# Local attention of a fused network on one core: scores on quarters of the array, and four reorderings

## The chip, the core and the metric

The kernel runs on one core of a Trainium2 chip. A core has TensorE (PE in the rows: matmuls; PEld is its weight loads), VectorE (DVE), ScalarE (ACT), GpSimd (POOL) and SyncE (SP), which here only issues DMAs. The engines run their own instruction lists and wait for each other through semaphores. PE reads SBUF and writes PSUM, eight banks of 512 float32 per partition. The metric is the device time of one execution in microseconds (us).

## What is computed

The reference is a token mixer, a linear attention and two feed-forward layers with local attention. The change touches the last part:

```python
def local_attention(q, k, v):                 # 8 heads of 64, window 128
    bk, bv = (look_around(bk), look_around(bv))       # previous window and this one: 256 keys
    sim = jnp.einsum('bhwid,bhwjd->bhwij', bq, bk)
    mask = (i < j) | (i > j + WINDOW) | (j == -1)
    attn = jax.nn.softmax(jnp.where(mask, -max, sim), axis=-1)
    return jnp.einsum('bhwij,bhwjd->bhwid', attn, bv)

def _layer(x, ...):
    q, k, v = split(shift_token(x) @ wqkv)
    q, k = rotary_xpos(l2norm(q) * qs, l2norm(k) * ksc)
    x = x + local_attention(q, k, v) @ wo
    h = layernorm(shift_token(x)) * lg + lb
    a, g = split(h @ w1 + b1)
    return x + (a * gelu(g)) @ w2 + b2        # two such layers, 4096 tokens
```

A query i of a window sees the keys i to 127 of the previous window and 0 to i of its own. `shift_token` takes the second half of the channels from the token before.

## The kernel before

The 4096 tokens are 32 tiles of 128. Each of the two layers is a local phase (attention, `local_phase`, line 964) and then an MLP phase (`mlp_phase`, line 1480). In the profile the local phases stand at about 634 to 1086 us and 1298 to 1745 us, the MLP phases behind them, and the token mixer and the linear attention ahead of the first.

**The local phase** is a software pipeline written by hand: `schedule` (line 1003) writes steps 0 to 3 out, loops over steps 4 to 31 in twos, and writes three draining steps out. In step n, PE (line 1399) does in this order, where a, b, c, d say which tiles exist: q and k of tile n (`project`, fp32r as three products each, L117 to L119, 12 matmuls), the transposes of q and then k of tile n-1 (L1412, 4 each), the transposes of the probabilities of pairs of heads 0 and 1 of tile n-2 (L1375, 4 each), v of tile n-1 (6 matmuls), pairs 2 and 3, the output product of tile n-3 (12 matmuls, ends with the semaphore y_full), two transposes of the next tile's x (L1349), four of the inverse row sums (L1394), the scores of tile n-1 (L1368), and probabilities times v of tile n-2 (L1385).

Scores of a pair of heads: each head has 64 rows (dimensions) of qT and kT, so that two heads lie in the two halves of the array's rows. One matmul is 64 rows by 128 queries with 256 moving keys; its head's result goes to a bank of its own. The profile counts each float32 matmul of this kind twice: the program lists 8 a tile, the trace 16. `kT` holds two windows in two slots; the tile's own keys are in slot 1 in every other step, and in slot 0 in the others. Pairs 0 and 1 go to the banks of q and k (QK, QK+1), pairs 2 and 3 to the banks of the transposes (TQ, TQ+1).

ACT in a step (line 1132): high part of the output (L1135), v (L1139), squares of q and k (L1143), qT and kT (L1147), the four copies of transposed probabilities (L1123), the high part of the next x (`x_hi`, L1105), copies of x, and at its end eight exponentials (L1117). DVE (line 1245): the rope products (L1265, L1270), sums of squares (L1273), the residual addition (L1192, waits for y_full), the low part of the next x (`x_lo`, L1182, L1184: it lets PE project that tile), and then eight masked row maxima (`score`, L1224) with ten steps of the norms' inverse square root between them (`rnorm`, L1233 to L1241). POOL adds the rope products (L1070) and multiplies by the norms (L1075): q first, then k; these release the transposes L1412. In layer 0 `late_stats` (line 1312), 19 short dependent DVE instructions for the last eight tiles' layer norm, stands between step 3 and the loop.

**The MLP phase** works on eight groups of four tiles. The shifted half of the channels comes back from memory: SP loads it for group g+1 while group g runs (`m_shifted`, L1529). SP first issues the next layer's weights and tables (L1518, L1520, layer 0 only).

Of the kernel before, what the change touches and what calls it, by code (L numbers as in the profile page):

```python
# [963 lines left out]
def local_phase(nc, s, mem, K, A, layer):  # L964
# [12 lines left out]
        (f"l{layer}_kT", [P, 2, LPAIRS, P], F32), (f"l{layer}_v", [P, 2, LINNER], F32),  # L977
# [39 lines left out]
    with nc.Block() as block:  # L1017
# [30 lines left out]
        def _(pool):  # L1048
# [3 lines left out]
            nc.gpsimd.memset(kt[:, 1], 0.0)  # L1052
# [38 lines left out]
        def _(act):  # L1091
# [39 lines left out]
            def step(n, r, a, b, c, d, piece=None):  # L1131
# [12 lines left out]
                if b:  # L1144
                    for k, dst in enumerate((qt[:], kt[:, 1 - r])):
                        wait(act, s.qk_t, 2 * (n - 1) + k + 1)
                        nc.scalar.activation(dst.rearrange("p m t -> p (m t)"), ps[:, TQ + k],  # L1147
# [6 lines left out]
                if a:  # L1154
                    x_hi(n + 1, 1 - r)
# [20 lines left out]
        def _(dve):  # L1176
# [67 lines left out]

            def step(n, r, a, b, c, d):
# [33 lines left out]
                if d and not drain(n, 2):  # L1279
                    add(n)  # L1280
                if a:
# [5 lines left out]
                    x_lo(n + 1, 1 - r)  # L1287
                for h in range(LH):
                    if b:
# [44 lines left out]
            schedule(dve, step, rebase, loop=late_stats)  # L1334
# [10 lines left out]
        def _(pe):  # L1345
# [53 lines left out]
            def step(n, r, a, b, c, d):  # L1399
                if a or b:  # L1400
                    wait(pe, s.x_done, n + 1)
                if a:
                    wait(pe, s.turned, n)
                    wait(pe, s.masked, 4 * (n - 1) - 2)
                    project(r, 0, QK)
                    project(r, 1, QK + 1).then_inc(s.qk_full.sem, 1)
                if b:
                    wait(pe, s.masked, 4 * (n - 1))
                    for k in range(2):
# [754 lines left out]
```

## Time and profile before

| | us |
|---|---|
| time, median of 3 runs (1953.76 to 1954.8) | 1953.86 |
| the profiled execution | 1955.45 |
| its span in the trace | 1953.7 |
| PE busy | 1863.4 |
| DVE busy | 1522.5 |
| ACT busy | 1094.7 |
| POOL busy | 431.3 |

The profiled execution is 1.6 us above the median and 1.75 us above its own span. A busy PE is not PE at its peak, since matmuls overlap in the records. The mean granted PE clock was 0.984 of full speed. The rows further below give a start (us from the span's start), a duration in us, the engine, the line, what is written from what, the shape, how many were merged (x) and, in brackets, the idle time of the engine before it and who ended it.

### The profile page before, as it was taken

What the parts mean: (1) busy time and instruction counts of PE and PEld (TensorE: products, weight loads), DVE (VectorE), ACT (ScalarE), POOL (GpSimd) and SP (SyncE); (2) the same over time, 40 slices, a digit from 0 to 9 for tenths busy, and PEclk for the clock granted to TensorE, in tenths of its full rate; (3) what the DMA queues carried; (4) which work ended last, traced back from release to release, by engine and by line L of the source; (5) the groups of instructions that cost most, each with busy time, mean ns of one, the idle gap of its engine ahead of it and who ended that gap; (6) DMA issues with size and microseconds to landing.
All of it is one profiled execution on the core that took longest, in us unless ns stands there. A gap on an engine that the chain in (4) does not pass through costs nothing. (4 is left out here: it accounts for less than half of the span.)

```text
span 1953.7 us, 40490 instructions
## 1 busy us (share of the span) xinstructions
PE 1863.4 (95%) x13340; PEld 1624.6 (83%) x13340; DVE 1522.5 (78%) x4717; ACT 1094.7 (56%) x2551; POOL 431.3 (22%) x319
## 2 busy tenths in 40 slices
PE   8899999999999799999998799979999999989998
PEld 8789889899898578888887688867888888878887
DVE  6888878878687688888887577768888888867777
ACT  4433433433432578888887334427787778853333
POOL 0000000000000335444543000013544454411010
PEclk9999999999999899999999899989999999999999
DMA  9100000000010100000000200010000000000002
GB/s 342 43 1 1 1 1 1 1 1 1 11 57 1 50 7 5 5 5 5 5 4 11 85 12 11 11 44 4 6 4 5 5 5 4 5 22 12 11 11 91
DMA packets 44980, 44.46 MB, mean 23 GB/s; under 512 B 8359, under 2 KB 39387, under 8 KB 44894
## 3 DMA queue, kind: packets, MB, share of 16 engines
q1 hardware_dynamic: 44894, 43.33, 6.7%
q8 instruction: 52, 0.85, 0.2%
q14 instruction: 34, 0.28, 0.0%
HBM read 34.93 MB, written 8.39 MB: 22 GB/s over the span
## 5 line engine op out<-in xcount | busy, mean ns | idle before, releaser
L1117 ACT ACTIVATE l_probs<-l_probs,l_negmax 128x256 f32<-128x256 f32 x512 | 253.2, 496 | 64.8 <-DVE l_negmax L1224 64.8
L1075 POOL TENSOR_TENSOR l_t<-l_t,l_rnorm 128x512 f32<-128x512 f32 x128 | 131.0, 1044 | 301.7 <-DVE l_rnorm L1241 301.7
L117 PE MATMUL ps<-local_w_hi,l_xT 128*128 128x512 f32 x384 | 167.5, 436 | 25.2 <-DVE l_xT L1184 16.1
L1070 POOL TENSOR_TENSOR l_t<-l_t,l_t 128x1024 f32<-128x1024 f32 x64 | 152.6, 2384 | 146.0 <-DVE l_t L1270 146.0
L1123 ACT ACTIVATE l_probsT<-ps 128x512 f32<-128x512 f32 x256 | 138.4, 594 | 40.3 <-PE ps L1375 40.2
L118 PE MATMUL ps<-local_w_lo,l_xT 128*128 128x512 f32 x384 | 155.5, 405 | 0.0
L119 PE MATMUL ps<-local_w_hi,l_xT 128*128 128x512 f32 x384 | 154.5, 402 | 0.0
L117 PE MATMUL ps<-m_hnT_hi,ffn_w_hi 128*128 128x512 f32 (+1 forms) x352 | 143.5, 408 | 10.4 <-DVE m_u L1642 6.1
L486 ACT ACTIVATE attn_exp<-ps 128x512 f32<-128x512 f32 x128 | 76.5, 600 | 133.1 <-PE ps L119 133.1
L1375 PE MATMUL ps<-ident,l_probs 128*128 128x128 f32 x1024 | 135.2, 276 | 6.2 <-ACT l_probsT L1123 6.2
L118 PE MATMUL ps<-m_hnT_lo,ffn_w_hi 128*128 128x512 f32 (+1 forms) x352 | 140.3, 399 | 0.0
L119 PE MATMUL ps<-m_hnT_hi,ffn_w_lo 128*128 128x512 f32 (+1 forms) x352 | 140.2, 398 | 0.0
L1375 PEld LDWEIGHTS ps<-ident,l_probs 128*128 128x128 f32 x1024 | 119.2, 142 | 16.1 <-ACT l_probsT L1123 5.9
L1368 PE MATMUL ps<-l_kT,l_qT 64*128 64x256 f32 x1024 | 127.9, 389 | 2.2 <-DVE l_t L1270 2.2
L1265 DVE TENSOR_TENSOR l_t<-ps,rope_c 128x1024 f32<-128x1024 f32 x64 | 78.4, 1224 | 65.6 <-ACT l_sq L1143 57.5
L1385 PEld LDWEIGHTS ps<-l_probsT,l_v 128*64 128x64 f32 x2048 | 110.5, 137 | 21.3 <-issue 21.3
L1050 POOL MEMSET l_xT<- 128x520 f32 x2 | 1.1, 531 | 571.5 <-POOLq L450 569.6
L1385 PE MATMUL ps<-l_probsT,l_v 128*64 128x128 f32 x2048 | 125.9, 276 | 0.3 <-DVE x L1192 0.3
L1581 ACT ACTIVATE m_gelu<-ps,ffn_b 128x512 f32<-128x512 f32 x80 | 55.1, 689 | 110.2 <-PE ps L119 110.2
L117 PEld LDWEIGHTS ps<-local_w_hi,l_xT 128*128 128x128 f32 x384 | 74.4, 194 | 49.2 <-DVE l_xT L1184 17.1
L1368 PEld LDWEIGHTS ps<-l_kT,l_qT 64*128 64x128 f32 x1024 | 94.0, 186 | 21.3 <-issue 13.1
L1568 ACT ACTIVATE m_u_hi<-m_u 128x512 fp32r<-128x512 f32 x80 | 50.6, 632 | 106.2 <-DVE m_u L1642 106.2
(252 smaller groups left out, 5823.5 us busy)
## 6 DMA issues: line engine op xcount, KB each, us to landing
tok_x<-x SPq DMA_DIRECT2D x16, 512.0 KB, 8.2
m_shifted<-shifted SPq DMA_DIRECT2D x20, 256.0 KB, 2.7
shifted<-x SPq DMA_DIRECT2D x64, 64.0 KB, 1.5
out<-x SPq DMA_DIRECT2D x8, 512.0 KB, 4.5
ffn_w_raw<-ffn_w SPq DMA_DIRECT2D x6, 640.0 KB
local_w_raw<-ffn_wqkv SPq DMA_DIRECT2D x4, 768.0 KB, 5.0
tok_base<-attn_base SPq DMA_DIRECT2D x4, 512.0 KB, 8.7
h<-txt SPq DMA_DIRECT2D x4, 512.0 KB, 8.4
```

Of the source, the lines that this page charges most:

```text
L117: nc.tensor.matmul(out, wh, mh, start=start, stop=False, skip_group_check=True)
L118: nc.tensor.matmul(out, wh, ml, start=False, stop=False, skip_group_check=True)
L119: return nc.tensor.matmul(out, wl, mh, start=False, stop=stop, skip_group_check=True)
L486: nc.scalar.activation(ex[:, at % 2], ps[:, at % 2], ACT.Exp).then_inc(s.attn_exp.sem, 1)
L1070: nc.gpsimd.tensor_tensor(t1[:], t1[:], t2[:], ALU.add).then_inc(s.summed.sem, 1)
L1075: nc.gpsimd.tensor_tensor(v, v, rn[:, a * LH:(a + 1) * LH].unsqueeze(2).to_broadcast([P, LH, DH]), ALU.mult).then_inc(s.rotated.sem, 1)
L1117: last = nc.scalar.activation(v, v, ACT.Exp, bias=nb[:, h:h + 1], scale=-1.0, accum_out=rsum[:, h:h + 1])
L1123: nc.scalar.activation(pt[:, pair], ps[:, PT[pair]], ACT.Copy).then_inc(s.p_done.sem, 1)
L1265: nc.vector.tensor_tensor(t1[:].rearrange("p a (h d) -> p a h d", d=DH), q, cw, ALU.mult)
L1368: last = nc.tensor.matmul(ps[:, bank + e, at:at + 2 * P], qt[rows, pair, :], kt[rows, :, pair, :], start=True, stop=True)
L1375: last = nc.tensor.transpose(ps[:, PT[pair], k * P:(k + 1) * P], pm[:, pair, k * P:(k + 1) * P], K.ident[:])
L1385: last = nc.tensor.matmul(ps[e * DH:(e + 1) * DH, OT, pair * P:(pair + 1) * P], vv[:, w, h * DH:(h + 1) * DH], pt[:, pair, (2 * e + w) * P ...
```

## The change

Five edits.

1. `score` works on quarters of the array: 64 rows by 64 queries. Queries 0 to 63 need 192 of the 256 keys, queries 64 to 127 another 192. Where the own window is in slot 1 these are in one piece (16 matmuls of 192 keys in the program, 32 in a trace); where it is in slot 0 they are two pieces of 128 and 64 (32 matmuls, 64 in a trace). `kT` is laid out pair by pair, its two slots side by side. What isn't written holds older numbers, which the mask covers.
2. The transposes of k come behind those of the first pair of probabilities. The waits for `qk_done` and `turned` move ahead of the inverses.
3. Steps 0 and 1: x_t, x_hi and x_lo of tile 1 come earlier, v of tile 0 is projected at the head of step 1, and DVE does x_lo and the first four row maxima of step 1 ahead of the norms.
4. `late_stats` runs ahead of step 0.
5. SP loads the first shifted group ahead of the next layer's weights.

```diff
-        (f"l{layer}_kT", [P, 2, LPAIRS, P], F32), (f"l{layer}_v", [P, 2, LINNER], F32),
+        (f"l{layer}_kT", [P, LPAIRS, 2, P], F32), (f"l{layer}_v", [P, 2, LINNER], F32),
...
@@ ACT, step
+                if a and isinstance(n, int) and n == 0:
+                    x_hi(n + 1, 1 - r)
                 if a:
                     wait(act, s.qk_full, n + 1)
...
@@ DVE, step
+                if a and one_of(n, 0):
+                    x_lo(n + 1, 1 - r)
                 if a:
                     wait(dve, s.squared, n + 1)
...
+                if one_of(n, 1):
+                    x_lo(n + 1, 1 - r)
+                    for h in range(LH // 2):
+                        if h == 0:
+                            wait(dve, s.scored, 1)
+                        score(0, h, mask)
...
-            schedule(dve, step, rebase, loop=late_stats)
+            late_stats()
+            schedule(dve, step, rebase)
...
@@ PE
-            def score(half):
+            def score(half, own):
...
+                reach = (((slice(0, 3 * DH),), (slice(DH, 4 * DH),)) if own else
+                         ((slice(2 * DH, 4 * DH), slice(0, DH)), (slice(0, 2 * DH), slice(3 * DH, 4 * DH))))
                 for pair in (2 * half, 2 * half + 1):
-                    for e in range(2):
-                        rows, at = slice(e * DH, (e + 1) * DH), pair % 2 * 2 * P
-                        last = nc.tensor.matmul(ps[:, bank + e, at:at + 2 * P], qt[rows, pair, :],
-                                                kt[rows, :, pair, :], start=True, stop=True)
+                    at = pair % 2 * 2 * P
+                    for part in range(len(reach[0])):
+                        for part_of_q in range(2):
+                            qs, keys = slice(part_of_q * DH, (part_of_q + 1) * DH), reach[part_of_q][part]
+                            for e in range(2):
+                                rows = slice(e * DH, (e + 1) * DH)
+                                last = nc.tensor.matmul(ps[qs, bank + e, at + keys.start:at + keys.stop], qt[rows, pair, qs],
+                                                        kt[rows, pair].rearrange("p w t -> p (w t)")[:, keys],
+                                                        start=True, stop=True)
...
@@ PE, step
+                if second:
+                    project(1 - r, 2, V).then_inc(s.v_full.sem, 1)
...
                     project(r, 0, QK)
+                    if first:
+                        x_t(n + 1, 1 - r)
                     project(r, 1, QK + 1).then_inc(s.qk_full.sem, 1)
                 if b:
                     wait(pe, s.masked, 4 * (n - 1))
...
+                    turned_t(n - 1, 0)
                 if c:
                     probs_t(n - 2, 0)
+                if b:
+                    turned_t(n - 1, 1)
...
@@ SP, MLP phase
+            shifted(0, 0)
             if not last_layer:
                 for dst, src in K.local_loads(layer + 1):
...
+            sp.wait_ge(*s.normed.room(2, 2))
+            shifted(1, 1)
+            with sp.Fori(1, NG // 2) as p:
```

`turned_t(t, k)` is the wait for `rotated` and the four transposes that stood in the loop over k.

PE in a step of the loop, behind the projection of q and k; l_t is the rotated q (first) and k, l_probs the probabilities. Before:

```order
L1412 MATMUL ps<-ident,l_t_8239 128x128 [waits s_l0_rotated]
L1412 MATMUL ps<-ident,l_t_8239 128x128 x3
L1412 MATMUL ps<-ident,l_t_8239 128x128 [waits s_l0_rotated]
L1412 MATMUL ps<-ident,l_t_8239 128x128 x3
L961 ISA
L1375 MATMUL ps<-ident,l_probs 128x128 [waits s_l0_exped]
L1375 MATMUL ps<-ident,l_probs 128x128 x3
```

And of the changed kernel:

```order
L1399 MATMUL ps<-ident,l_t_8239 128x128 [waits s_l0_rotated]
L1399 MATMUL ps<-ident,l_t_8239 128x128 x3
L961 ISA
L1405 MATMUL ps<-ident,l_probs 128x128 [waits s_l0_exped]
L1405 MATMUL ps<-ident,l_probs 128x128 x3
L961 REGISTER_ALU
L1399 MATMUL ps<-ident,l_t_8239 128x128 [waits s_l0_rotated]
L1399 MATMUL ps<-ident,l_t_8239 128x128 x3
```

Four transposes of probabilities now stand between those of q and those of k.

PE at the end of a step of the loop, from the inverses (l_spread) to probabilities times v. Before, every step:

```order
L1394 MATMUL ps<-ident,l_spread 128x128 [waits s_l0_p_done,s_l0_spread]
L1394 MATMUL ps<-ident,l_spread 128x128 x3
L1368 MATMUL ps<-l_kT,l_qT 128x256 [waits s_l0_turned,s_l0_qk_done]
L1368 MATMUL ps<-l_kT,l_qT 128x256 x7
L1385 MATMUL ps<-l_probsT,l_v 64x128 [waits s_l0_y_done,s_l0_v_done]
```

The changed kernel, in a step with the own window in slot 1:

```order
L1424 MATMUL ps<-ident,l_spread 128x128 [waits s_l0_spread,s_l0_p_done,s_l0_turned,s_l0_qk_done]
L1424 MATMUL ps<-ident,l_spread 128x128 x3
L1391 MATMUL ps<-l_kT,l_qT 64x192 x16
L1415 MATMUL ps<-l_probsT,l_v 64x128 [waits s_l0_y_done,s_l0_v_done]
L1415 MATMUL ps<-l_probsT,l_v 64x128 x15
```

In the steps between, the row of 16 is eight rows that alternate between 64x128 x4 and 64x64 x4. The inverses carry the scores' waits too.

SP at the head of the MLP phase of layer 0. Before:

```order
L1518 DMA local_w_raw<-ffn_wqkv 128x1536 x2
L1518 DMA local_w_raw<-ffn_wo 128x4x256
L1520 DMA rope_c<-rope_cos 128x1024
L1520 DMA rope_s<-rope_sin 128x1024
L1520 DMA l_qkscale<-ffn_q_scale 128x64
L1520 DMA l_qkscale<-ffn_k_scale 128x64
L1521 UNCONDITIONAL_BRANCH
L1521 ISA
L1529 ISA [waits s_rows_stored1,s_rows_stored0,s_m0_normed]
L1529 DMA m_shifted<-shifted 128x4x128
```

And of the changed kernel:

```order
L1554 DMA m_shifted<-shifted 128x4x128 [waits s_rows_stored1,s_rows_stored0]
L1560 DMA local_w_raw<-ffn_wqkv 128x1536 x2
L1560 DMA local_w_raw<-ffn_wo 128x4x256
L1562 DMA rope_c<-rope_cos 128x1024
L1562 DMA rope_s<-rope_sin 128x1024
```

The first shifted group stands ahead of the seven loads instead of behind them.

## Rows read from the trace of the kernel before

**Rows 1.** Timeline of PE, one step of layer 0's loop.
```profile
909.79 2.00 PE L1368 MATMUL ps<-l_kT,l_qT 64*128 64x256 f32 x16
911.72 1.97 PE L1385 MATMUL ps<-l_probsT,l_v 128*64 128x128 f32 x32
913.62 0.50 PE L117 MATMUL ps<-local_w_hi,l_xT 128*128 128x512 f32 x1
...
916.51 1.09 PE L1412 MATMUL ps<-ident,l_t 128*128 128x128 f32 x8
917.44 1.04 PE L1375 MATMUL ps<-ident,l_probs 128*128 128x128 f32 x8
918.24 0.48 PE L117 MATMUL ps<-local_w_hi,l_xT 128*128 128x512 f32 x1
...
919.71 1.03 PE L1375 MATMUL ps<-ident,l_probs 128*128 128x128 f32 x8
920.50 0.36 PE L117 MATMUL ps<-local_w_hi,l_oT_hi 128*128 128x256 f32 x1
...
921.89 0.28 PE L119 MATMUL ps<-local_w_hi,l_oT_lo 128*128 128x256 f32 x1
...
922.76 2.00 PE L1368 MATMUL ps<-l_kT,l_qT 64*128 64x256 f32 x16
```

**Rows 2.** Timeline of PE in the linear attention: float32 matmuls on the whole array.
```profile
170.37 1.51 PE L848 MATMUL ps<-attn_kv,attn_qT 128*128 128x130 f32 x12
```

**Rows 3.** Timeline of DVE, the same step as rows 1.
```profile
909.36 0.42 DVE L1192 TENSOR_TENSOR x<-ps,x 128x256 f32 x1 [0.64 <-PE ps L119]
910.98 0.42 DVE L1224 CUSTOM_DVE_ANT_0 l_probs<-ps,mask_odd 128x256 f32<-128x256 f32 x1
922.33 0.42 DVE L1192 TENSOR_TENSOR x<-ps,x 128x256 f32 x1 [0.66 <-PE ps L119]
```

**Rows 4.** Timeline of ACT, the same step.
```profile
911.88 0.51 ACT L1117 ACTIVATE l_probs<-l_probs,l_negmax 128x256 f32<-128x256 f32 x1 [0.57 <-DVE l_negmax L1224]
...
918.69 1.06 ACT L1123 ACTIVATE l_probsT<-ps 128x512 f32<-128x512 f32 x2
```

**Rows 5.** Timeline of POOL, the same step.
```profile
914.85 2.05 POOL L1075 TENSOR_TENSOR l_t<-l_t,l_rnorm 128x512 f32<-128x512 f32 x2 [4.78 <-DVE l_rnorm L1241]
```

**Rows 6.** Timeline of DVE and PE, layer 0: late statistics, and who waits.
```profile
690.27 0.16 DVE L151 TENSOR_REDUCE l_rstd<-h_stats 128x8 f32<-128x16 f32 x1
...
695.05 0.17 DVE L1316 SCALAR_TENSOR_TENSOR l_shift<-l_mean,l_rstd 128x8 f32<-128x8 f32 x1
...
696.66 0.50 PE L117 MATMUL ps<-local_w_hi,l_xT 128*128 128x512 f32 x1 [3.13 <-ACT l_v L1139]
```

**Rows 7.** Timelines: first steps, DVE of layer 0, then POOL, DVE and PE of layer 1.
```profile
642.84 1.23 DVE L1265 TENSOR_TENSOR l_t<-ps,rope_c 128x1024 f32<-128x1024 f32 x1 [5.87 <-ACT l_sq L1143]
...
1315.22 2.04 POOL L1075 TENSOR_TENSOR l_t<-l_t,l_rnorm 128x512 f32<-128x512 f32 x2 [2.56 <-DVE l_rnorm L1241]
...
1320.49 1.22 DVE L1265 TENSOR_TENSOR l_t<-ps,rope_c 128x1024 f32<-128x1024 f32 x1 [5.23 <-PE ps L1412]
...
1328.03 0.47 PE L117 MATMUL ps<-local_w_hi,l_xT 128*128 128x512 f32 x1 [2.98 <-DVE l_negmax L1224]
```

**Rows 8.** Timelines: MLP phases of layers 0 and 1, SP, DVE and PE.
```profile
1090.94 1.11 SPq L1529 DMA_DIRECT2D m_shifted<-shifted  x2
...
1098.70 0.87 DVE L1613 BATCH_NORM_STATS2 m_stats<-m_shifted 128x6 f32<-128x128 f32 x4 [10.63 <-DMA m_shifted<-shifted]
...
1086.96 0.47 PE L117 MATMUL ps<-m_hnT_hi,ffn_w_hi 128*128 128x512 f32 x1 [2.14 <-PEq L1017]
...
1137.59 1.09 PE L1708 MATMUL ps<-ident,m_hn 128*128 128x128 f32 x8 [1.41 <-DVE m_hn L1621]
...
1745.86 0.47 PE L117 MATMUL ps<-m_hnT_hi,ffn_w_hi 128*128 128x512 f32 x1 [2.13 <-PEq L1017]
...
1787.95 1.09 PE L1708 MATMUL ps<-ident,m_hn 128*128 128x128 f32 x8 [0.15 <-DVE m_hn L1621]
```

More of the change, by code:

```diff
@@ L1154, in step @@
                 if a:
-                    x_hi(n + 1, 1 - r)
+                    if not (isinstance(n, int) and n == 0):
+                        x_hi(n + 1, 1 - r)
                     x_copy((n + 2) % T, r)
@@ L1243, in _, with one_of @@
             LAST = 10
+            def one_of(n, *steps):
+                return isinstance(n, int) and n in steps
             def step(n, r, a, b, c, d):
@@ L1286, in step @@
                     chain.mark(rnorm(2))
-                    x_lo(n + 1, 1 - r)
+                    if not one_of(n, 0, 1):
+                        x_lo(n + 1, 1 - r)
                 for h in range(LH):
-                    if b:
+                    if b and not (one_of(n, 1) and h < LH // 2):
                         if h % 4 == 0:
@@ L1399, in step @@
             def step(n, r, a, b, c, d):
+                first, second = (isinstance(n, int) and n == k for k in range(2))
                 if a or b:
                     wait(pe, s.x_done, n + 1)
+                if second:
+                    project(1 - r, 2, V).then_inc(s.v_full.sem, 1)
                 if a:
@@ L1408, in step @@
                     wait(pe, s.masked, 4 * (n - 1))
-                    for k in range(2):
-                        wait(pe, s.rotated, 2 * n - 1 + k)
-                        for m in range(LPAIRS):
-                            last = nc.tensor.transpose(ps[:, TQ + k, m * P:(m + 1) * P], t1[:, k, m * P:(m + 1) * P],
-                                                       K.ident[:])
-                        last.then_inc(s.qk_t.sem, 1)
+                    turned_t(n - 1, 0)
                 if c:
                     probs_t(n - 2, 0)
+                if b:
+                    turned_t(n - 1, 1)
+                if c:
                     wait(pe, s.r_out, n - 2)
                     probs_t(n - 2, 1)
-                if b:
+                if b and not second:
                     wait(pe, s.v_done, n - 1)
@@ L1432, in step @@
                     last.then_inc(s.y_full.sem, 1)
-                if a:
+                if a and not first:
                     if c:
@@ L1436, in step @@
                     x_t(n + 1, 1 - r)
+                if b:
+                    wait(pe, s.qk_done, 2 * n)
+                    if a:
+                        wait(pe, s.turned, n + 1)
                 if c:
@@ L1441, in step @@
                 if b:
-                    wait(pe, s.qk_done, 2 * n)
-                    if a:
-                        wait(pe, s.turned, n + 1)
-                    score(0)
-                    score(1)
+                    score(0, 1 - r)
+                    score(1, 1 - r)
                 if c:
@@ L1515, in _, with shifted @@
         def _(sp):
+            for k in range(2):
+                sp.wait_ge(*K.rows_stored[k].after(16 * (layer + 1) * T // 2))
+            def shifted(g, r):
+                sp.dma_start(sh[:, 1 - r], A.scratch[bass.ds((g + 1) % NG * GT, GT), :]
+                             .rearrange("(j p) c -> p j c", p=P)).then_inc(s.sh_in[1 - r].sem, 16)
+            shifted(0, 0)
             if not last_layer:
@@ L1520, in _ @@
                     sp.dma_start(dst, src).then_inc(K.local_s[layer + 1].const_in.sem, 16)
-            with sp.Fori(0, NG // 2) as p:
+            sp.wait_ge(*s.normed.room(2, 2))
+            shifted(1, 1)
+            with sp.Fori(1, NG // 2) as p:
                 for r in range(2):
-                    g = 2 * p + r
-                    sp.wait_ge(*s.normed.room(g + 1, 2))
-                    if r == 0:
-                        for k in range(2):
-                            sp.wait_ge(*K.rows_stored[k].after(16 * (layer + 1) * T // 2))
-                    sp.dma_start(sh[:, 1 - r], A.scratch[bass.ds((g + 1) % NG * GT, GT), :]
-                                 .rearrange("(j p) c -> p j c", p=P)).then_inc(s.sh_in[1 - r].sem, 16)
+                    sp.wait_ge(*s.normed.room(2 * p + r + 1, 2))
+                    shifted(2 * p + r, r)
             sp.wait_ge(*s.normed.room(NG + 1, 2))
```

11 lines of the change are left out of this document (8 added, 3 removed).

## The prediction

> **What bounds the kernel now.** I read the page's engine table first: PE is busy 1863.4 of 1953.7 us, the others far less. The timeline of PE in one step of the local loop shows where the time goes [rows 1]: between two score stages, 909.79 and 922.76, lie 12.97 us and not one bracket of idle time. The local loop is bound by PE's own work, so a shorter matmul stage shortens the step until something else is late. 32 tiles a layer give 29 steps a layer in this steady state and 58 in all. Outside them PE does wait, and each wait is a place of its own: late statistics in layer 0 [rows 6], the first two steps of each layer [rows 7], the first group of layer 0's MLP [rows 8].
>
> **What a float32 matmul costs here.** On the whole array, 12 instructions of 130 columns take 1.51 us with the last one's latency [rows 2], some 0.11 each when that is left out: about 0.85 ns a column, two cycles of the 2.4 GHz clock. A score instruction of 256 columns would so stream 0.217 us, and 16 one behind the other 3.47. The stage takes 911.72 − 909.79 = 1.93 [rows 1]: the two heads' halves of the rows stream at the same time, 8 × 0.217 = 1.73, and 0.20 is not streaming. Values, in two halves of the columns, say the same: 32 instructions of 128 columns (0.108) take 913.62 − 911.72 = 1.90, which is 16 × 0.108 = 1.73 and 0.17.
>
> **Edit 1, scores on quarters.** In a step with the own window in slot 1: 32 instructions of 192 columns, 0.163 each. Four at once, that is 8 × 0.163 = 1.30, and with 0.19 beside it 1.49. In the steps between, 64 instructions of 128 and 64 columns, mean 96: 16 × 0.081 = 1.30 again. Each stage loses **0.44** of 1.93. That row halves run together is seen, that column halves do is seen; both together is not. If only two of the four run together, the stage is 16 × 0.163 + 0.19 = 2.80. These are the ends of the unknown, −0.44 and +0.87 a step; I take −0.44, since each half of the claim has its row and both stages come out of one rule.
>
> The Trainium skill bears on this in "TensorEngine Tiling (Array Packing)", Tiling Modes: 64 by 64 gives four independent tiles. The rows agree for two; no row of this trace shows four. The same page (Instruction Overhead) speaks against the edit: each matmul carries some 60 cycles, so a tiling shouldn't be taken from a dimension that is small already. As an estimate from it, 64 × 0.025 = 1.6 us would be a floor in every other step, 1.79 with the rest: a gain of 0.14 there.
>
> **What is late next.** The loop that closes through the softmax. From DVE's addition, 909.36, the first row maximum comes at 910.98 [rows 3], the first exponential at 911.88, and ACT is then dense: the copies of the probabilities of pairs 0 and 1 stand without idle time ahead of them and end at 918.69 + 1.06 = 919.75 [rows 4]. PE's transposes of pairs 2 and 3 begin at 919.71; pair 3's four, at 919.71 + 0.44 = 920.15 (half of the eight and their successor's start at 920.50 [rows 1]), write the bank that the second of the copies empties. The slack is 920.15 − 919.75 = 0.40, and a wake-up takes of it what DVE's addition shows, 922.33 after PE's last product began at 921.89 and took 0.28 [rows 1, 3]: 0.16. So of 0.44 only about 0.24 is surely free, and up to 0.34 if part of the wake-up overlaps. I take **0.28 a step**: 58 × 0.28 = 16.2 us. Ends: 0, if something else closes at once, and 0.44.
>
> **Edit 2, k's transposes later.** POOL's second product (k) ends at 914.85 + 2.05 = 916.90; the eight transposes began at 916.51, so k's four come at about 916.97 and are only just in time [rows 1, 5]. With 0.44 off the step, PE would stand there about 0.3. Now four transposes of probabilities lie between, 0.4 of PE work (918.24 − 917.44 = 0.80 for eight, 0.4 for four [rows 1]), which covers it. Without that cover edit 1 would lose 0.3 a step, 17 us. The copies of kT come 0.4 later on ACT, which has other copies to do first. The inverses now wait for `turned` and `qk_done`; behind them PE queues the scores and values, but the scores waited for these already, and neither wait shows as idle time ahead of 909.79 [rows 1]. I cost it at nothing; bounds −0.3 to +0.1 a step, the upper inside the range below.
>
> **Edit 4, late statistics.** From 690.27 to 695.05 + 0.17 is 4.95 us of DVE, and PE waits 3.13 for it at 696.66 [rows 6]. The gain lies between; I take **4.4**, nearer the upper, since DVE carries its lateness into the row maxima behind. In the new place DVE has 5.87 idle before 642.84 [rows 7], so that 4.95 fits if it can begin at once. It is queued behind loads, whose landing no row gives; I charge 1.1 (ends 0 and 4.0) to layer 0's first steps.
>
> **Edit 3, first two steps.** In layer 1 POOL's product for tile 0 ends at 1315.22 + 2.04 = 1317.26, but DVE's rope of tile 1 begins at 1320.49, released by PE's transposes [rows 7]. These stand behind tile 1's projection, which waited for x_lo. With that gone, eight transposes (917.44 − 916.51 = 0.93 [rows 1]) would end at 1318.2: 2.3 earlier. The wait of 2.98 at 1328.03 for a row maximum [rows 7] shrinks with it or not at all: ends 0 and 5.3. I take 2.3 in layer 1 and 2.3 − 1.1 = 1.2 in layer 0, **3.5**.
>
> **Edit 5, shifted group first.** In layer 0 DVE waits 10.63 us for m_shifted, whose load SP issued at 1090.94 behind seven others; from PE's first projection, 1086.96, to the transposes at 1137.59 are 50.63. Layer 1, with nothing ahead of that load, needs 1787.95 − 1745.86 = 42.09 [rows 8]. The difference, **8.5**, is the gain. The weights are wanted only some 160 us on. Ends 7 and 9.
>
> **Ends of the phases.** Three tiles a layer are outside the 29 steps; their scores are shorter too, at most 3 × 0.44. I take 0.4 a layer, 0.8.
>
> **Sum.** 16.2 + 4.4 + 3.5 + 8.5 + 0.8 = 33.4. The profiled execution took 1955.45, so 1922.05; the median lies 1.6 lower: 1920.4, say **1920**. Without the steady steps the other terms are 17.2.
>
> **Rivals.**
> (B) *The softmax loop doesn't bind.* Each step gains 0.44: 58 × 0.16 = 9.3 more, 1911. For: ACT's order could absorb the lateness; against: ACT has no idle time between 911.88 and 919.75 [rows 4].
> (C) *The steady gain is eaten,* by that loop or by k's transposes: 1920.4 + 16.2 = 1937.
> (D) *Slower: two tiles at a time.* The score stage becomes 2.80 instead of 1.93, 58 × 0.87 = 50.5 more, less 17.2: about 1987. It decides from a stage of 1.93 + 17.2 / 58 = 2.23 on. For: no row has both halvings at once. Against: nothing in either stage's arithmetic sets rows and columns apart.
> (E) *Slower: a cost per instruction.* Values come at 1.90 / 32 = 0.059 each [rows 1]. If that is an issue limit and not streaming, 64 instructions take 3.8, 1.87 more in 29 steps, while 32 take 1.9 as before: 54 − 17.2 = +37, about 1991. Against: streaming explains the values without it.
> "TensorE: Matmul & The Clock Gate", Part 2 (decode and dispatch), in the Trainium skill has such a cost, about 62 ns a matmul when the sequencer decodes in its own code, else it is far less. By it the 64 take an estimated 4.0; the values' spacing agrees with it and with streaming alike, so the trace doesn't decide.
> (F) *The edits at the ends don't do what they say:* the first steps find another wait (DVE's idle before 1320.49 stays), and the load is late for its rows. Half of 17.2 goes: 1929.
>
> **How the numbers follow.** The forecast has 0.62, with its own range 1912 to 1928 (0.1 a step either way is 6 us, the ends 2 to 3). B 0.09, C 0.09, D 0.09, E 0.05, F 0.06. All but D and E are faster. A measurement of this kernel can tell about 0.2% (4 us) from no change. Faster 0.85, same 0.02, slower 0.13. From 1909 to 1938 the range takes in the forecast, B, F and C; D and E, 0.14, stay out.
>
> **What would show it.** Score stage, start to start: 1.49 in every step (D: 2.8; E: 3.8 in every other). Step period 12.69; PE idle for ACT's copies of l_probsT ahead of the second four of the later probability transposes, some 0.15; none ahead of k's. DVE's 19 instructions ahead of the loop, 3.13 gone. Rope of tile 1 some 2 us earlier against its layer's start. m_shifted's wait near 2 us, and the stretch to L1708's match near 42. The forecast is wrong if the period stays at 12.97 with a short score stage (C), or if any stage is longer than 1.93.

## The result

The changed kernel takes 1932.95 us (median of 4 runs, 1932.06 to 1933.62) against 1954.33 for the kernel before on the same chip: a ratio of 0.9889, 95% interval 0.9876 to 0.9902. It is 21 us faster. The forecast said 1920 and 33 us; 1933 lies inside its range of 1909 to 1938, and about two thirds of the forecast gain came. The span in the trace went from 1953.7 to 1930.6.

Timeline of PE in the changed kernel, one step of layer 0's loop, as [rows 1] (start, duration, engine, line, what from what, merged count):

```profile
902.97 1.53 PE L1391 MATMUL ps<-l_kT,l_qT 64*64 64x192 f32 x32
904.43 1.97 PE L1415 MATMUL ps<-l_probsT,l_v 128*64 128x128 f32 x32
...
909.19 0.66 PE L1399 MATMUL ps<-ident,l_t 128*128 128x128 f32 x4
909.68 0.60 PE L1405 MATMUL ps<-ident,l_probs 128*128 128x128 f32 x4
910.19 0.65 PE L1399 MATMUL ps<-ident,l_t 128*128 128x128 f32 x4
910.68 0.60 PE L1405 MATMUL ps<-ident,l_probs 128*128 128x128 f32 x4
911.03 0.47 PE L117 MATMUL ps<-local_w_hi,l_xT 128*128 128x512 f32 x1
...
912.64 1.13 PE L1405 MATMUL ps<-ident,l_probs 128*128 128x128 f32 x8
913.52 0.36 PE L117 MATMUL ps<-local_w_hi,l_oT_hi 128*128 128x256 f32 x1
...
915.78 1.57 PE L1391 MATMUL ps<-l_kT,l_qT 64*64 64x128 f32 x64
917.28 0.98 PE L1415 MATMUL ps<-l_probsT,l_v 128*64 128x128 f32 x14
```

Start to start the score stage takes 904.43 − 902.97 = 1.46 us with 32 instructions and 917.28 − 915.78 = 1.50 with 64; it was 1.93. The step takes 915.78 − 902.97 = 12.81, the next one 12.88. So 0.45 left the score stage and only 0.12 left the step. Two places on PE took the rest: the sixteen transposes from 909.19 to 911.03 take 1.84 where they took 918.24 − 916.51 = 1.73 [rows 1], and from the v projection's start at 911.03 to the output product's at 913.52 are 2.49 where 920.50 − 918.24 = 2.26 were [rows 1].

The three single places answer to [rows 6 to 8]. The changed kernel: late statistics now in the first steps of layer 0 (DVE), the first transposes of q and the projection of tile 2 in layer 1 (PE), and the first group of the MLP in layer 0 (SP, DVE, PE).

```profile
639.24 0.17 DVE L151 TENSOR_REDUCE l_rstd<-h_stats 128x8 f32<-128x16 f32 x1 [1.09 <-DMA mask_odd<-mask_prev]
...
642.90 0.17 DVE L1332 SCALAR_TENSOR_TENSOR l_shift<-l_mean,l_rstd 128x8 f32<-128x8 f32 x1
...
1299.60 0.66 PE L1399 MATMUL ps<-ident,l_t 128*128 128x128 f32 x4 [2.75 <-POOL l_t L1075]
...
1308.25 0.47 PE L117 MATMUL ps<-local_w_hi,l_xT 128*128 128x512 f32 x1 [0.99 <-DVE l_negmax L1227]
...
1079.29 0.39 SPq L1554 DMA_DIRECT2D m_shifted<-shifted  x1
1079.32 0.47 PE L117 MATMUL ps<-m_hnT_hi,ffn_w_hi 128*128 128x512 f32 x1 [2.14 <-PEq L1017]
1082.10 0.87 DVE L1651 BATCH_NORM_STATS2 m_stats<-m_shifted 128x6 f32<-128x128 f32 x4 [1.66 <-DMA m_shifted<-shifted]
...
1121.19 1.09 PE L1746 MATMUL ps<-ident,m_hn 128*128 128x128 f32 x8 [1.41 <-DVE m_hn L1659]
```

DVE's wait for m_shifted fell from 10.63 to 1.66 us, and the stretch 1121.19 − 1079.32 is 41.87 where 50.63 were. The wait of 2.98 ahead of tile 2's projection in layer 1 is 0.99.

Set out by stretches of the two traces (start of the first projection, score stages, start of the MLP), the 23.1 us of the span are these. Here and below differences are taken before rounding:

| stretch | before | after | gain |
|---|---|---|---|
| all ahead of the first local projection | 637.0 | 638.2 | −1.2 |
| layer 0, to the fourth score stage | 65.2 | 59.1 | 6.1 |
| layer 0, 27 steps of the loop | 350.2 | 346.9 | 3.2 |
| layer 0, last steps, to the MLP | 34.5 | 35.0 | −0.5 |
| MLP of layer 0, to layer 1's first projection | 213.8 | 205.0 | 8.8 |
| layer 1, to the fourth score stage | 62.3 | 59.8 | 2.5 |
| layer 1, 27 steps | 350.1 | 347.1 | 3.1 |
| layer 1, last steps, to the MLP | 32.7 | 33.4 | −0.8 |
| MLP of layer 1 and output | 207.8 | 206.0 | 1.8 |

The first line is no effect of the change: nothing ahead of it was touched, and over all the kernels below it lies between 633.8 and 639.2. So differences of 2 us between two totals say little here, and the stretches are compared instead. Even a stretch isn't exact: from layer 1's first projection to its fourth score stage the changed kernel took 59.8 us, and e9_loads_first, the same program there, 58.9.

### The profile page after: what moved, and what is told of

It is laid out like the page before. It is cut to its first block and busy times, and to the rows that moved or that the text cites. A ratio compares the mean times of both kernels' runs of the same rounds, so it can differ in the third digit from the quotient of the medians.

```text
span 1930.6 us, 44672 instructions
## 1 busy us (share of the span) xinstructions
PE 1853.2 (96%) x15388; PEld 1602.9 (83%) x15388; DVE 1529.3 (79%) x4715; ACT 1094.2 (57%) x2551; POOL 431.8 (22%) x319
## 5 line engine op out<-in xcount | busy, mean ns | idle before, releaser
L1405 PE MATMUL ps<-ident,l_probs 128*128 128x128 f32 x1024 | 151.5, 282 | 5.8 <-ACT l_probsT L1123 5.4
L117 PE MATMUL ps<-attn_w_hi,attn_xT_hi 128*128 128x512 f32 x256 | 106.9, 418 | 3.7 <-PEq L185 2.1
L1227 DVE CUSTOM_DVE_ANT_0 l_probs<-ps,mask_even 128x256 f32<-128x256 f32 x256 | 106.8, 419 | 0.0
L1227 DVE CUSTOM_DVE_ANT_0 l_probs<-ps,mask_odd 128x256 f32<-128x256 f32 x256 | 106.3, 419 | 0.1
```

Source lines behind the costliest of these rows:

```text
L117: nc.tensor.matmul(out, wh, mh, start=start, stop=False, skip_group_check=True)
L1227: last = nc.vector.tensor_tensor_reduce(pm[:, pair, e * 2 * P:(e + 1) * 2 * P], ps[:, bank, at:at + 2 * P], mask[:], -8.0, -LOWEST, ALU.ad ...
L1405: last = nc.tensor.transpose(ps[:, PT[pair], k * P:(k + 1) * P], pm[:, pair, k * P:(k + 1) * P], K.ident[:])
```

## Experiments

### First set: which loop holds the step

Two explanations stood against each other. S: the softmax loop through ACT, as forecast, is shorter than PE's work by less than thought. T: PE loses it itself, in four groups of transposes instead of two. Each kernel is the changed one with one edit.

**e1_halves** undoes edit 1.

```diff
-                        for part_of_q in range(2):
-                            qs, keys = slice(part_of_q * DH, (part_of_q + 1) * DH), reach[part_of_q][part]
-                            ... ps[qs, bank + e, at + keys.start:at + keys.stop], qt[rows, pair, qs], ...[:, keys]
+                    for e in range(2):
+                        ... ps[:, bank + e, at:at + 2 * P], qt[rows, pair, :], kt[rows, pair].rearrange("p w t -> p (w t)")
```

> The changed kernel with edit 1 undone: scores again on halves of the rows, 256 keys each, all else as changed. Theory S (in the changed kernel the step of 12.85 us is set by the softmax loop: DVE's addition, first row maximum, ACT's exponentials and what it does behind them without a pause, second copy of the probabilities, pair 3's transposes, output product): with the long score stage PE is the limit again, the step is 12.97 to 13.03 and the time 1933 + 58 x 0.15, about 1941. Theory T (the missing gain is lost in PE's own order, by the transposes in four groups of four, 0.10 us a step): the step is 12.97 + 0.10 = 13.07 and the time about 1945, slower still if the waits ahead of pairs 2 and 3 stay too.

**e2_k_back** undoes edit 2 as far as the order of the transposes goes.

```diff
                     turned_t(n - 1, 0)
+                    turned_t(n - 1, 1)
                 if c:
                     probs_t(n - 2, 0)
-                if b:
-                    turned_t(n - 1, 1)
```

> The changed kernel with edit 2 undone: k's four transposes right behind q's, inverses still with the scores' waits. Theory S with POOL's product close behind: PE stands some 0.5 us ahead of k's transposes, since the product for k comes at the same moment as before; pair 2's transposes then begin 0.2 later than ACT alone would allow, the step is 13.0 to 13.1, the time about 1943. Theory T: the four groups are the loss, so that it goes with this: step about 12.75, time about 1927.

**e3_act_order** changes ACT's order.

```diff
+                if c:
+                    for pair in range(2):
+                        probs_out(n - 2, pair)
                 if b:
                     for k, dst in enumerate((qt[:], kt[:, :, 1 - r])):
...
                 if c:
-                    for pair in range(LPAIRS):
+                    for pair in (2, 3):
                         probs_out(n - 2, pair)
```

> The changed kernel with one change in ACT's order: the copies of the probabilities of pairs 0 and 1 ahead of those of qT and kT, instead of behind. Theory S: pairs 2 and 3 no longer wait for ACT; the next limit is POOL's product for k and then PE itself, step 12.5 to 12.6, time 1933 - 58 x 0.27, about 1917. Theory T: nothing in PE's order changes, so the step stays at 12.85 and the time at 1933.

**e4_act_order_k_last** adds PE's order probabilities 0, probabilities 1, k.

```diff
                     probs_t(n - 2, 0)
-                if b:
-                    turned_t(n - 1, 1)
-                if c:
                     wait(pe, s.r_out, n - 2)
                     probs_t(n - 2, 1)
+                if b:
+                    turned_t(n - 1, 1)
```

> As e3_act_order, and k's transposes behind the probabilities of pairs 0 and 1 both. Theory S: PE's own work alone is left, 12.97 - 0.47 = 12.50 a step, time about 1913; the slower, if qT and kT come so late that the scores wait for them (PE would then show it ahead of the inverses). Theory T: one group boundary less, step 12.80, time 1930.

| kernel | median us | ratio to before, 95% | step, mean of 27, us |
|---|---|---|---|
| before | 1957.0 | | 12.97 |
| changed (its own comparison) | 1932.95 | 0.9889 (0.9876 to 0.9902) | 12.85 |
| e1_halves | 1934.0 | 0.9885 (0.9861 to 0.9910) | 12.91 |
| e2_k_back | 1930.7 | 0.9875 (0.9855 to 0.9896) | 12.86 |
| e3_act_order | 1932.1 | 0.9875 (0.9854 to 0.9896) | 12.86 |
| e4_act_order_k_last | 1930.95 | 0.9875 (0.9856 to 0.9894) | 12.85 |

Both explanations fall. e3 freed pairs 2 and 3 from ACT, and the step stayed; so S isn't what holds it. e2 has the transposes in their old order, and the step stayed; so T isn't either. Where PE's or ACT's order is changed, PE's lost time turns up in another place and the step is 12.85 to 12.86. In e3, for example, the v projection and the transposes of pairs 2 and 3 take 911.79 − 909.52 = 2.27 us instead of 2.49, but from the projection of q and k to the transposes of q are 907.67 − 904.61 = 3.06 instead of 909.19 − 906.33 = 2.86. Something that none of these kernels touches has that period.

The rows that show it are of POOL and DVE. First of the kernel before: POOL's addition of the rope products, and DVE's first instruction of the norms, in the step of [rows 3]. They were not among the rows that the forecast read.

```profile
907.68 2.39 POOL L1070 TENSOR_TENSOR l_t<-l_t,l_t 128x1024 f32<-128x1024 f32 x1 [2.29 <-DVE l_t L1270]
909.70 0.39 DVE L1233 TENSOR_SCALAR l_ss<-l_ss 128x16 f32<-128x16 f32 x1
```

Then the same two of the changed kernel, with the first row maximum, the first exponential, the squares, the rope product and the next addition of POOL:

```profile
901.05 2.38 POOL L1070 TENSOR_TENSOR l_t<-l_t,l_t 128x1024 f32<-128x1024 f32 x1 [2.29 <-DVE l_t L1279]
902.54 0.42 DVE L1195 TENSOR_TENSOR x<-ps,x 128x256 f32 x1 [0.44 <-PE ps L119]
902.88 0.58 DVE L1236 TENSOR_SCALAR l_ss<-l_ss 128x16 f32<-128x16 f32 x1
904.22 0.42 DVE L1227 CUSTOM_DVE_ANT_0 l_probs<-ps,mask_odd 128x256 f32<-128x256 f32 x1
905.11 0.51 ACT L1117 ACTIVATE l_probs<-l_probs,l_negmax 128x256 f32<-128x256 f32 x1 [0.63 <-DVE l_negmax L1227]
...
908.09 2.04 POOL L1075 TENSOR_TENSOR l_t<-l_t,l_rnorm 128x512 f32<-128x512 f32 x2 [4.66 <-DVE l_rnorm L1244]
...
910.06 1.01 ACT L1145 ACTIVATE l_sq<-ps 128x1024 f32<-128x1024 f32 x1
911.36 1.23 DVE L1274 TENSOR_TENSOR l_t<-ps,rope_c 128x1024 f32<-128x1024 f32 x1 [0.68 <-ACT l_sq L1145]
913.86 2.39 POOL L1070 TENSOR_TENSOR l_t<-l_t,l_t 128x1024 f32<-128x1024 f32 x1 [1.48 <-DVE l_t L1279]
```

And of e3 and of e4 the pair again:

```profile
899.53 2.39 POOL L1070 TENSOR_TENSOR l_t<-l_t,l_t 128x1024 f32<-128x1024 f32 x1 [2.29 <-DVE l_t L1282]
901.16 0.79 DVE L1239 TENSOR_SCALAR l_ss<-l_ss 128x16 f32<-128x16 f32 x1
```

```profile
898.58 2.37 POOL L1070 TENSOR_TENSOR l_t<-l_t,l_t 128x1024 f32<-128x1024 f32 x1 [2.30 <-DVE l_t L1282]
900.07 0.92 DVE L1239 TENSOR_SCALAR l_ss<-l_ss 128x16 f32<-128x16 f32 x1
```

An instruction on 16 numbers a partition takes 0.39, 0.58, 0.79 and 0.92 us. It ends at 910.09, 903.46, 901.95 and 900.99, and POOL's addition ended at 910.07, 903.43, 901.92 and 900.95: it ends 0.02 to 0.04 behind POOL each time, wherever it began. The more PE's end of the loop gets ahead, the longer it stands. The same holds in all 54 steps of the two loops, in the kernel before, the changed one and e1 to e4: the instruction ends 0.03 to 0.04 us behind POOL's addition. That closes a ring in which PE has no part: POOL's addition, norms' first instruction, first row maximum, exponentials, squares, rope products, POOL's addition. In the changed kernel it goes from 901.05 to 913.86, 12.81 us, the length of the step. The Trainium skill has the rule, "SBUF — State Buffer", Who interferes with whom: DVE and GpSimd share a pair of SBUF ports that one instruction holds for its whole length, and a DVE tensor_scalar can take the mode that needs the pair. The four rows agree with it.

### Second set: the ring through POOL, or a loop through its products

R is this ring. P is another loop over POOL: scores, row maxima with the norms between them, POOL's product for q, PE's transposes of q, and so on to the next scores.

**e5_half_add** shortens POOL's addition. It leaves out the addition of the two rope products for k.

```diff
-                nc.gpsimd.tensor_tensor(t1[:], t1[:], t2[:], ALU.add).then_inc(s.summed.sem, 1)
+                nc.gpsimd.tensor_tensor(t1[:, 0], t1[:, 0], t2[:, 0], ALU.add).then_inc(s.summed.sem, 1)
```

> As e4_act_order_k_last, but POOL adds the rope products of q alone; k's half of the addition is left out, so POOL's instruction of 2.38 us becomes about 1.2. All four runs before had a step of 12.85 (12.91 with halves) whatever PE's and ACT's order, and in each DVE's first norm instruction ended 0.03 us behind POOL's addition. Theory R (the ring is POOL's addition, DVE's first norm instruction, which doesn't run before POOL is done, first row maximum, exponentials, squares, rope products, POOL's addition again): the ring gets 1.2 shorter, PE is the limit, step 12.5, time 1931 - 58 x 0.35, about 1911. Theory P (the ring is PE, row maxima, norms, POOL's product for q, PE's transposes): POOL's addition isn't in it, the step stays at 12.85 and the time at 1931.

**e6_max_first** changes DVE's order and keeps all the rest of the changed kernel.

```diff
-                    chain(rnorm(0))
-                    wait(dve, s.rotated, 2 * n)
-                    chain(rnorm(1))
-                    chain.mark(rnorm(2))
                     if not one_of(n, 0, 1):
                         x_lo(n + 1, 1 - r)
                 for h in range(LH):
...
+                        for k in ((0, 1), (2, 3), (4, 5), (6,), (7,), (8,), (9,), (10,))[h]:
+                            ... rnorm(k)
```

> The changed kernel, whole, with DVE's order changed in one place: row maxima begin ahead of the norms, and the eleven norm instructions stand between them (two behind each of the first three). Theory R: the wait for POOL's addition leaves the ring; the first maximum comes at once when the scores are there, some 0.15 to 0.2 earlier. ACT's copies and POOL's product for k, now two norm instructions later, come next: step 12.65 to 12.8, time 1922 to 1931. Theory P: the norms end later by about 0.4, the product with them, step 13.0 or more, 1942.

**e7_k_last_max_first** is e4 with e6's order on DVE.

> e4_act_order_k_last and e6's order on DVE together. Theory R: PE alone, or POOL's product for q by about 0.1: step 12.5 to 12.65, time 1911 to 1920. Theory P: q's transposes wait for the product that is 0.4 later, step 13.0 or more.

**e8_probs_first_max_first** is e7 with another order on PE:

```diff
+                if c:
+                    probs_t(n - 2, 0)
+                    wait(pe, s.r_out, n - 2)
+                    probs_t(n - 2, 1)
                 if b:
                     wait(pe, s.masked, 4 * (n - 1))
                     turned_t(n - 1, 0)
+                    turned_t(n - 1, 1)
```

> As e7_k_last_max_first, but on PE the transposes of the first two pairs of probabilities stand ahead of those of q and k, so that POOL's products have 0.8 us more. Theory R: PE alone, 12.5 a step, time about 1911. If this is no shorter than e7, POOL's product wasn't the next limit.

| kernel | median us | ratio to before, 95% | step, us |
|---|---|---|---|
| before | 1955.2 | | 12.97 |
| e5_half_add | 1904.0 | 0.9733 (0.9715 to 0.9752) | 12.46 |
| e6_max_first | 1949.1 | 0.9965 (0.9951 to 0.9978) | 13.12 |
| e7_k_last_max_first | 1928.7 | 0.9867 (0.9850 to 0.9884) | 12.81 |
| e8_probs_first_max_first | 1911.7 | 0.9783 (0.9763 to 0.9803) | 12.54 |

e5 shows R. Its kernel doesn't compute the whole, since k's rope sum is missing, but only its time is read. With an addition of 1.29 us instead of 2.38 DVE's instruction is 0.17 long, and PE has no idle time in the step. Timeline of e5, POOL, DVE and PE:

```profile
891.10 1.29 POOL L1070 TENSOR_TENSOR l_t<-l_t,l_t 128x512 f32<-128x512 f32 x1 [2.58 <-DVE l_t L1282]
892.26 0.42 DVE L1198 TENSOR_TENSOR x<-ps,x 128x256 f32 x1
892.60 0.17 DVE L1239 TENSOR_SCALAR l_ss<-l_ss 128x16 f32<-128x16 f32 x1
```

```profile
880.17 1.57 PE L1394 MATMUL ps<-l_kT,l_qT 64*64 64x128 f32 x64
...
892.69 1.37 PE L1394 MATMUL ps<-l_kT,l_qT 64*64 64x192 f32 x28
```

One piece of POOL's work, which PE waits for nowhere by name, is worth 27 us against e4: 58 × (12.85 − 12.46) = 22.6 in the steady steps, the rest in the first ones. 12.46 is PE's own work: 12.97, less 0.45 of the score stage and 0.06 of the order of the transposes (e1: 12.97 − 12.91).

e6 shows that P is real and close behind. R's expectation of a gain was wrong there, P's of a loss right. Timeline of e6:

```profile
908.32 0.42 DVE L1195 TENSOR_TENSOR x<-ps,x 128x256 f32 x1 [0.46 <-PE ps L119]
...
909.71 0.42 DVE L1227 CUSTOM_DVE_ANT_0 l_probs<-ps,mask_odd 128x256 f32<-128x256 f32 x1 [0.37 <-issue]
...
913.88 0.17 DVE L1244 SCALAR_TENSOR_TENSOR l_rnorm<-l_tmp,l_rnorm 128x16 f32<-128x16 f32 x1
914.19 2.05 POOL L1075 TENSOR_TENSOR l_t<-l_t,l_rnorm 128x512 f32<-128x512 f32 x2 [4.99 <-DVE l_rnorm L1244]
...
915.29 0.66 PE L1398 MATMUL ps<-ident,l_t 128*128 128x128 f32 x4 [0.17 <-POOL l_t L1075]
```

The first maximum comes 909.71 − 908.32 = 1.39 us after DVE's addition instead of 904.22 − 902.54 = 1.68, but the product starts 914.19 − 908.32 = 5.87 after it instead of 908.09 − 902.54 = 5.55, and the transposes of q wait for it. 0.32 late, 0.27 lost a step. e7, with an order of transposes that asks for k later but for q as early, gains 0.04 on the changed kernel and no more; that was foreseen by neither R (12.5 to 12.65) nor P (13.0). e8 asks for both later, behind the first two pairs of probabilities. Then PE shows no idle time in the step, which is 12.54, and the whole is 21 us faster than the changed kernel and 43 faster than the one before. Part of these 21 is its early start, 633.8 us to the first local projection against 638.2; the 27 steps of each layer alone are 8.4 and 8.6 us shorter.

### Third set: the other edits, and one step further

**e9_loads_first** puts `shifted(0, 0)` behind the seven loads again.

> The changed kernel with edit 5 undone: the first shifted group stands behind the next layer's seven loads again. Forecast of the sum: 8.5 us lost in the first group of layer 0's MLP, which goes back from 41.9 to about 50.5 us, time 1933 + 8.5 = 1941.5. Rival: a part of the 8.8 us seen there was PE's clock (granted 0.59 in the first 4 us before, 1.00 after), which doesn't depend on the load; then the stretch is about 49.0 and the time 1940.

**e10_late_stats_back** puts `late_stats` between step 3 and the loop.

> The changed kernel with edit 4 undone: late_stats between step 3 and the loop again. By the sum: the step around it grows by 4.4, layer 0's first steps get up to 1.1 shorter, so +3.3 to +4.4, time about 1937. Rival: the 19 instructions delay layer 0's first steps by as much as they cost behind step 3, and the time stays at 1933.

**e11_first_steps_back** takes out what edit 3 did to steps 0 and 1, on PE, ACT and DVE.

> The changed kernel with edit 3 undone, late_stats staying ahead of step 0. By the sum and by the traces (from the first projection to the fourth score stage 45.75 us in layer 1 with the edit, 49.31 minus the two shorter score stages' 0.3 without): +2.2 to +3.3 in layer 1 and +1.3 to +2.3 in layer 0, time 1936.5 to 1938.5. Rival: late_stats hid only because of this edit, and layer 0 loses 4 more: 1942.

**e12_flag_later** is e8 with the last instruction of `x_lo` (the multiplication by the flag) behind the third row maximum.

> As e8_probs_first_max_first, with x_lo's last small DVE instruction, 0.67 us long in e8 since it ended only with POOL's addition, behind the third row maximum. Theory R: the last instruction ahead of the maxima that waits for POOL is gone; e8's step of 12.54 has PE without idle time, PE's own work is 12.48, so that no more than 0.06 a step can come: 12.48 to 12.54, time 1908 to 1912. Rival: POOL's lateness still reaches PE and 0.1 or more a step come, 1905.

| kernel | median us | ratio to before (1954.0), 95% | the stretch, us, against the changed kernel |
|---|---|---|---|
| e9_loads_first | 1942.5 | 0.9944 (0.9927 to 0.9960) | MLP of layer 0: 214.5 against 205.0 |
| e10_late_stats_back | 1934.9 | 0.9905 (0.9889 to 0.9922) | layer 0 to the fourth scores: 64.4 against 59.1 |
| e11_first_steps_back | 1934.7 | 0.9899 (0.9882 to 0.9915) | the same: 60.3 against 59.1; layer 1: 61.9 against 59.8 |
| e12_flag_later | 1917.1 | 0.9805 (0.9789 to 0.9822) | step 12.60; e8 12.54 |

e9: edit 5 is worth 9.5 us, by the total and by the stretch. The first group, from PE's first projection to the transposes, takes 51.3 us; its rival had 49.0. Its row, DVE waiting again:

```profile
1090.99 0.87 DVE L1651 BATCH_NORM_STATS2 m_stats<-m_shifted 128x6 f32<-128x128 f32 x4 [11.31 <-DMA m_shifted<-shifted]
```

What it costs holds a part of PE's clock: over the first 25 us of this MLP the mean granted clock is 0.80 in e9, as in the kernel before, and 1.00 in the changed one. In e1, e10 and e11, which all keep edit 5, it is 0.93 and the MLP takes 206.5. So edit 5 is worth 9.5 against 205.0, and 213.8 − 206.5 = 7.3 if one compares the kernel before with those that have its low clock at the head.

e10: edit 4 is worth 5.2 at its place, and e11: edit 3 is worth 1.1 and 2.1, 3.2 together. Both totals moved by no more than 2, with intervals of ± 3 us. In e10 more than half of the 5.2 is missing in the total. The trace has it elsewhere: its start is 1.4 earlier, and from the end of layer 0's loop to the end of its MLP it takes 1.1 less, with the mean granted clock at 1.00 in the last steps and 0.93 at the head of the MLP where the changed kernel has 0.84 and 1.00; the clock comes next. The two edits' values rest on the stretches alone, and with the 0.8 by which a stretch can differ, edit 3's two figures are rough. The rival for e11, that late statistics would no longer be hidden, is out: layer 0 lost 1.1.

e12 made e8 no better, and by its step 0.06 worse; the totals, 5.4 us apart, don't say more, since the starts of the two traces alone differ by 4.3. In e8 the flag's instruction takes 0.67 us and ends 0.04 behind POOL's addition (892.18 + 0.67 = 892.85, 890.43 + 2.38 = 892.81); in its new place it takes 0.22. But the first row maximum comes no sooner, 911.99 − 910.66 = 1.33 us after DVE's addition instead of 892.76 − 891.40 = 1.36, and the fourth comes 914.02 − 911.99 = 2.03 after the first instead of 894.66 − 892.76 = 1.90, with the flag between them. That one frees the bank into which PE projects at 914.51:

```profile
914.02 0.42 DVE L1235 CUSTOM_DVE_ANT_0 l_probs<-ps,mask_even 128x256 f32<-128x256 f32 x1
```

```profile
914.51 0.50 PE L117 MATMUL ps<-local_w_hi,l_xT 128*128 128x512 f32 x1
```

That the maximum ends at about the time of the projection is read; that PE waited for it and nothing else isn't marked in the row. Of the versions that compute the whole, e8 is the fastest.

### The clock at a layer's end

The granted clock is the share of its full speed that TensorE is allowed. The ends of the layers lost 0.5 and 0.8 where 0.8 were to be gained in all, and the last MLP gained 1.8 that nobody had asked for. They belong together. Busy time by stretch, before and then after (length, busy PE, PEld, DVE, ACT and POOL, granted PE clock, DMA share, GB/s), from layer 1's last score stage to the MLP and the first 14 us of the MLP:

```profile
1727.00:1745.90 18.90, 12.72 (x134) 10.91 (x133) 12.38 (x39) 10.18 (x27) 1.04 (x1) 1.00 0.04 11
1745.90:1760.00 14.10, 14.10 (x60) 11.60 (x61) 8.39 (x32) 4.70 (x7) 0.00 (x0) 0.88 0.13 38
```

```profile
1703.60:1724.60 21.00, 14.79 (x150) 12.92 (x149) 13.17 (x43) 10.28 (x27) 1.04 (x1) 0.84 0.04 10
1724.60:1739.00 14.40, 14.13 (x72) 11.82 (x72) 9.79 (x37) 5.71 (x8) 0.00 (x0) 1.00 0.13 38
```

PE waits 2.7 us for ACT's copies of the last tile's probabilities in both. Before, the clock stayed at 2.4 GHz through the last steps and was low (0.88 on the mean) at the head of the MLP; after, it is low in the last steps (0.84) and full in the MLP. The last steps take 2.1 longer and the MLP 1.8 less. In the step ahead of these rows it is the other way round: 1713.2 to 1727.0 before has 0.88 and takes 13.8 us, 1691.2 to 1703.6 after has 1.00 and takes 12.4. The clock is at 1.2 or 2.4 GHz, so that a mean of 0.88 over 13.8 us means 2 × 0.12 × 13.8 = 3.3 us at the lower level. Worked out so, both kernels spend 6.7 us at it around layer 1's end: before in two pieces, one of them in the MLP, and after in one, in the last steps. The amount is the same, and it has moved from one row of the table to others. e1_halves, which differs from the changed kernel in the score stage alone, has 18.9 us from its last scores to the MLP in both layers, as the kernel before had in layer 1. A single stretch moves by up to 2 us by this. What decides where the clock falls stays open.

## Why the prediction was right or wrong

**The price of the matmuls: right.** Four quarters run at the same time, and a column costs what the halves said: 1.49 forecast, 1.46 and 1.50 measured. Rivals D (2.80) and E (3.8 in every other step) are out. Twice as many instructions cost 0.04 us. The estimate from the Trainium skill, "TensorEngine Tiling (Array Packing)", Instruction Overhead, was 1.79 for the stage of 64; the measurement disagrees with it.

**What is late next: wrong, and the whole miss.** The term was 58 × 0.28 = 16.2; the steps gave 0.12, 58 × 0.12 = 7. The step that failed is the one that took 910.98 − 909.36 = 1.62, from DVE's addition to the first row maximum, for a fixed length that moves along with the addition. It isn't: 0.2 of it was a small instruction that stood until POOL was done, and when the addition comes earlier against POOL, that instruction gets longer. The loop was read along the chain of data, and what it shared with another engine wasn't in it. How much room the ring left is in the rows of the kernel before. The last small instruction ahead of the first row maximum, before and then in the changed kernel:

```profile
910.78 0.16 DVE L1184 TENSOR_SCALAR l_xT<-l_xT 128x2 fp32r<-128x2 f32 x1
```

```profile
904.15 0.16 DVE L1187 TENSOR_SCALAR l_xT<-l_xT 128x2 fp32r<-128x2 f32 x1
```

The maximum began 910.98 − 910.78 = 0.20 after it before, and 904.22 − 904.15 = 0.07 in the changed kernel. On the mean of the 54 steps it is 0.22 and 0.10. So before, DVE stood about 0.12 there; it isn't marked for what, but the maximum reads the scores, which had begun at 909.79. The ring had that much room and no more, 12.97 − 0.12 = 12.85, and 0.12 was all that a shorter score stage could give, at 0.45 or at any other figure. e5 gives the proof: with half of POOL's addition the step is 12.46, 0.39 less than e4's with the whole of it, and 0.51 less than before, where rival B had 0.44. The part on ACT was not false but not the next limit either: pairs 2 and 3 do wait for ACT in the changed kernel, and e3, without that wait, is as slow. The period is neither the 12.69 of the forecast nor the unchanged 12.97 that the forecast named as its refutation.

**Edit 2: its price of nothing was right, its value wrong.** "Without that cover edit 1 would lose 0.3 a step, 17 us": e2 loses nothing. PE does stand ahead of k's transposes there, and no longer ahead of pairs 2 and 3, because the ring sets the step in either case. With the old score stage, where PE is the limit, the new order is worth 12.97 − 12.91 = 0.06 a step (e1). The transposes take 1.84 and not 1.73 in the changed kernel, since k's start at 910.19, when POOL's product for k has just ended, 908.09 + 2.04 = 910.13. PE's row in e2:

```profile
908.28 0.66 PE L1399 MATMUL ps<-ident,l_t 128*128 128x128 f32 x4 [0.20 <-POOL l_t L1075]
```

**Edit 4: right, without its charge.** 4.4 forecast, 5.2 by e10. The 1.1 charged to layer 0's first steps for the loads ahead of it didn't come. DVE begins at 639.24, after 1.09 us of waiting for mask_odd, but the first rope products start 644.11 − 638.20 = 5.91 us after the first projection, and 642.70 − 636.76 = 5.94 in e10, where nothing stands ahead of them.

**Edit 3: right in the sum, in part by luck,** 3.5 forecast, 3.2 by e11. In layer 1 it was 2.3 against 2.1. DVE's rope products of tile 1 began 19.7 us after layer 1's first projection before and 17.5 in the changed kernel, 2.2 earlier as forecast; but e11 has 18.5, so only 1.0 of that is edit 3's. PE's wait of 7.08 us for x_lo ahead of tile 1's projection is gone, and in its place stand 2.18 for DVE and 2.75 for POOL, ahead of the first transposes; the wait of 2.98 for a row maximum fell by 2.0. In layer 0 it was 1.2 against 1.1, but the 1.2 was 2.3 less a charge that never came.

**Edit 5: right,** 8.5 forecast, 8.8 in the two traces, 9.5 by e9, 7.3 against the kernels with the clock low at the MLP's head. e9 moves nothing but the load's place in SP's queue, so that is the cause; the size depends by 2 us on the clock, which the forecast didn't speak of.

**The ends: wrong in sign,** +0.8 forecast, −1.3 measured, with the granted clock lower in the last steps of both layers (0.84 against 0.92 and 1.00). With the 1.8 that came back in the last MLP it is 0.5.

Together: 7 + 5 + 3 + 9 + 0.5, less the start that was 1.2 later, make the 23 us of the span. The terms outside the steady steps were 17.2 in the forecast and are about 17.5 here. The measured time lies in the range because the range took in rival C, no steady gain at all, which was nearer in mechanism than the forecast, and nearer in time: 1937 against 1920, and 1933 measured.

## What to carry to other kernels

When a stage on the busiest engine gets shorter, the next limit can be a ring that doesn't pass through it. Look for it among small instructions that are longer than others of their size: here one of 16 elements that took 0.4 us, where 0.17 is its length, was waiting though the profile calls it busy, and its end beside another engine's end told for what. And try the order of the engines that wait together: the maxima first cost 16 us by themselves (e6), and with two changes of order that cost and brought nothing by themselves (e3, e4) and one more they brought 21.

## What the runs showed of the hardware

Four 64 by 64 tiles of float32 matmuls run at once at the rate that halves had: 32 instructions of 192 columns in 1.46 us, 64 of 96 on the mean in 1.50. A DVE TENSOR_SCALAR on 16 elements between SBUF operands doesn't finish while POOL's TENSOR_TENSOR runs: 0.17 us long without it (e5), up to 0.92 with it, and its end is POOL's to 0.04. One on 2 elements does the same (0.67 in e8, 0.22 in e12). In the same rows DVE's additions that read PSUM keep their 0.42 us under POOL's addition. Over the last steps of layer 1 the mean granted clock was 0.84 in the changed kernel and 1.00 in e1, with the same 2.7 us without matmuls in them and a step that differs by 0.06 us.
